# Three attention stages: operand rows loaded in runs of 24, 16 and 8 partitions, and the sums over the values taken once per key tile

## The chip, the cores and the metric

The kernel runs on one core of a Trainium2 chip. Its engines are TensorE (PE, matmuls; PEld its weight loads), VectorE (DVE), ScalarE (ACT), GpSimd (POOL) and SyncE (SP, which here issues all DMAs). The metric is the device time of one execution in microseconds (us), the median of several.

## What is computed

A chain of eight layers on x of 4 x 1024 tokens of 128 features. Three are attentions with 16 heads of 8 features; the others are mixtures of experts, a fast-weight layer and low-rank layers, which the diff does not touch. The three attentions, cut to their core:

```python
# a: linear biases                                   (4 batches, 16 heads, 1024 x 1024 scores)
scores = einsum('bqhd,bkhd->bhqk', q, k) / sqrt(8) + slopes[h] * -abs(i - j)
out = einsum('bhqk,bkhd->bqhd', softmax(scores), v)
# b: scores damped by distance
scores = einsum('bhsd,bhtd->bhst', q, k) / sqrt(8) * exp(-abs(decay) * abs(i - j))
# c: no projection, x minus its mean over time is query and key, x itself the value
corr = softmax(einsum('bthd,bThd->bhtT', xc, xc)); out = einsum('bhtT,bThd->bthd', corr, xh)
```

## The kernel before

**Operands.** Scores are taken from bf16 numbers at nearly f32 precision: each f32 query and key is split into three bf16 parts (0 coarse, 1 middle, 2 fine), and six products of parts are added. So a head's operand has 6 x 8 = 48 rows (`ROWS`), one block of 8 rows for each entry of `Q_PARTS` and `K_PARTS`. The parts are made in `project_qkv` (stages a and b) and `centre_and_split` (c), stored to DRAM in `parts_dram`, and loaded from there into `q_rows` and `k_rows`, four heads (`GH`) side by side. The 48 rows are there twice, at partitions 0 and 64 (`PAIR_ROW`), so that two matmuls of 64 rows run beside each other in PE.

**Loads.** In `attend_transposed` SP loads the operands of a group (one batch, four heads) while the group before it is worked on; `half` is one of two buffers. It waits on `o_out`, the copies of the sums of the group that used the buffer before, and issues one DMA for each block of 8 rows, for k and for q and for both places: 24 DMAs, of 64 KB mostly, and two more for bias rows (a) or shift rows (c).

**The attention's loop.** `attend_transposed` works on 16 groups a stage. A group has 8 key tiles J of 128 keys, a key tile has 4 units (one head each), so 32 units n. For a unit, PE computes a score tile of 128 keys x 1024 queries (`scores`, L741, two matmuls, one for each half c of the queries) into one of 3 slots of PSUM (`SLOTS`). In a and b DVE then adjusts the 512 columns in the half that holds the keys (L831, L828), and signals `adjusted`. ACT takes the exponential of the tile (L804) into `probs`. When all four heads of a key tile are there, PE multiplies the values with them (`sum_up`, L760), into one PSUM bank for each half c; an f32 matmul shows as two instructions in the trace, so one half of a key tile is 8 instructions. At the end of a group DVE copies both banks out (`take_sums`, L817).

**The order on PE** is written out in `batch`: at unit n first `scores` of unit n + 3, which waits until the exponential of unit n has freed the slot, then sums. Half 0 of a key tile is summed at its last unit (n % 4 == 3), half 1 two units later, except for the last key tile of a group, where both are taken at once:

```python
if n % GH == GH - 1:
    sum_up(hg, n // GH, 0, b)
    if n + 1 == UNITS:
        sum_up(hg, n // GH, 1, b)
if n % GH == 1 and n > GH:
    sum_up(hg, n // GH - 1, 1, b)
```

In stage a `alibi_span` leaves out scores far from the diagonal for the heads with steep slopes: heads 0 to 3 keep narrow spans, heads 8 to 15 are full. The function `attend` is another route for wide scores; this execution does not take it.

Of the kernel before, what the change touches and what calls it, by code (L numbers as in the profile page):

```python
# [16 lines left out]
BF16 = mybir.dt.bfloat16  # L17
# [4 lines left out]
D = 128  # L22
BATCH, SEQ = 4, 1024
# [5 lines left out]
CHUNK = 512  # L29
# [151 lines left out]
Q_PARTS = (0, 0, 1, 1, 0, 2)  # L181
K_PARTS = (0, 1, 0, 1, 2, 0)
# [6 lines left out]
def project_qkv(nc, tag, XT, w_qkv, b_qk, b_v, V, parts_dram, scale, head_of, longest2, damp=None):  # L189
# [8 lines left out]
    with ExitStack() as stack:  # L198
# [105 lines left out]
        def _(act):  # L304
            for x in range(SPLITS + 1):
                b = x % RING
                if x < SPLITS:
                    u, v = divmod(x, VERS)
                    act.wait_ge(biased, x + 1)
                    if x >= RING:  # L310
                        act.wait_ge(stored[b], 16 * (x // RING))
                    act.copy(parts[:, b, 0, :], full[:, b, :]).then_inc(part1, 1)
                    if v == 0:
                        if u >= 2 * RING:
                            act.wait_ge(norm2_done, u // 4 - 1)
                        act.activation(squares[:, u % (2 * RING), :], full[:, b, :], ACT.Square).then_inc(squared, 1)
# [13 lines left out]
        def _(sp):  # L330
            for x in range(SPLITS):
# [3 lines left out]
                sp.dma_start(parts_dram[v, w].rearrange("s f t -> f s t")[:, :, c * CHUNK:(c + 1) * CHUNK],  # L335
                             parts[:, x % RING, :, :]).then_inc(stored[x % RING], 16)
            for b in range(RING):
                sp.wait_ge(stored[b], 16 * (SPLITS // RING))
# [68 lines left out]
def attend(nc, tag, V, operands, parts_dram, tables, op, out_all, ident):  # L407
# [7 lines left out]
    with ExitStack() as stack:  # L415
# [36 lines left out]
        def _(sp):  # L452
            with sp.Fori(0, HEADS // GH) as hg:
                with sp.Fori(0, BATCH // 2) as bp:
                    for half in range(2):

                        sp.wait_ge(group_done, hg * 4 + bp * 2 + (half + 1))
                        for rows, which, order in ((q_rows, 0, Q_PARTS), (k_rows, 1, K_PARTS)):
                            for n, part in enumerate(order):
                                src = parts_dram[0, which, part].rearrange("(h e) t -> e h t", e=HD)  # L460
# [183 lines left out]
def attend_transposed(nc, tag, V, operands, parts_dram, out_t, ident, shift_dram=None, table=None, slopes=None,  # L644
# [23 lines left out]
    with ExitStack() as stack:  # L668
# [14 lines left out]
        LOADS = 4 * len(Q_PARTS) + 2 * (bias_dram is not None or shift_dram is not None)  # L683

        @block.sync
        def _(sp):
            with sp.Fori(0, BATCH) as b:
                for hg in range(HG):
                    half, hs, at = hg % 2, slice(hg * GH, (hg + 1) * GH), bass.ds(b * SEQ, SEQ)
                    sp.wait_ge(o_out, b * (2 * HG) + (2 * hg + 2))  # L690
                    for tile in range(2):
                        for n, (qp, kp) in enumerate(zip(Q_PARTS, K_PARTS)):
                            rows = slice(PAIR_ROW * tile + n * HD, PAIR_ROW * tile + (n + 1) * HD)
                            version = far * tile
                            q_src = parts_dram[version, 0, qp].rearrange("(h e) t -> e h t", e=HD)
                            k_src = parts_dram[version, int(by_dve), kp].rearrange("(h e) t -> e h t", e=HD)
                            sp.dma_start(k_rows[rows, half, :, :], k_src[:, hs, at]).then_inc(loaded[half], 16)
                            if by_dve:
                                sp.dma_start(q_rows[rows, half, :, :], q_src[:, hs, at]).then_inc(loaded[half], 16)
                            else:  # L700
                                sp.dma_start(q_rows[rows, half, :, tile * SIDE:(tile + 1) * SIDE],
                                             q_src[:, hs, bass.ds(b * SEQ + tile * SIDE, SIDE)]
                                             ).then_inc(loaded[half], 16)
# [20 lines left out]
        def _(pe):  # L724
# [42 lines left out]
            def batch(b, final):  # L767
                for hg in range(HG):
                    for n in range(UNITS):
# [8 lines left out]
                        if n % GH == GH - 1:  # L778
                            sum_up(hg, n // GH, 0, b)
                            if n + 1 == UNITS:  # L780
                                sum_up(hg, n // GH, 1, b)
                        if n % GH == 1 and n > GH:
                            sum_up(hg, n // GH - 1, 1, b)
# [384 lines left out]
def centre_and_split(nc, tag, XT, parts_dram, shift_dram, head_of):  # L1168


    with ExitStack() as stack:
# [69 lines left out]
        def _(sp):  # L1241
            for b, c in enumerate(cut):
                sp.wait_ge(part3, b + 1)
                sp.dma_start(parts_dram[0, 0].rearrange("s f t -> f s t")[:, :, c], parts[:, :, c]).then_inc(stored, 16)
# [3 lines left out]
            sp.wait_ge(stored, 16 * 2 * BATCH)  # L1248
# [1046 lines left out]
def build(nc, t, out, stages=8, first=0):  # L2295
    with ExitStack() as stack:
# [3 lines left out]
        parts_dram = nc.dram_tensor("qk_parts", [2, 2, 3, D, TOK], BF16, kind="Internal").ap()  # L2300
# [96 lines left out]
```

## Time and profile before

| | |
|---|---|
| median of 3 runs | 3687.84 us (3684.51 to 3689.68) |
| the profiled execution, its own time | 3692.91 us |
| its span, first to last instruction | 3691.2 us |
| PE busy | 2983.0 us (81%) |
| ACT busy | 2362.0 us (64%) |
| DVE busy | 2264.1 us (61%) |
| POOL busy | 471.1 us (13%) |
| mean granted clock of PE | 0.909 |
| DMA | 107.70 MB, mean 29 GB/s |

The busy share of an engine is an average over eight layers with different limits, so a stage has to be read by itself. The stages touched here lie at 126 to 690 us (a), 1372 to 1892 us (b) and 3133 to 3608 us (c). PE's clock has two levels, 1.2 GHz (0.5 in the profile) and 2.4 GHz (1.00).

### The profile page before, as it was taken

To read this page: it belongs to the slowest core of one execution; us is meant where nothing else is said; L and a number is where in the kernel's file an instruction comes from. 1 tells how busy PE (TensorE), PEld (TensorE's weight loads), DVE (VectorE), ACT (ScalarE), POOL (GpSimd) and SP (SyncE) were. 2 spreads that over 40 slices of the span, in tenths; PEclk is the share of its full clock that TensorE was granted. 3 is DMA by queue.
4 is the path that set the end of the run, shared out by engine and by line. 5 is a ranking of instruction groups with operands and counts; after the bars stand their busy time and mean duration, and the time that the engine had idled before them with its cause. 6 is when DMAs were issued, how large, how long until landed. Compare 5 with 4: busy or idle time off the path is not lost. (4 is left out here: it accounts for less than half of the span.)

```text
span 3691.2 us, 56232 instructions
## 1 busy us (share of the span) xinstructions
PE 2983.0 (81%) x18300; PEld 1343.0 (36%) x18300; DVE 2264.1 (61%) x3797; ACT 2362.0 (64%) x3466; POOL 471.1 (13%) x320
## 2 busy tenths in 40 slices
PE   4588888799999438888879999968886842999997
PEld 2111212366666311111136666632235640111115
DVE  6466666677777657666666777767779966000004
ACT  5577777455444539988955544455533344999993
POOL 5000000000000330000000000026544422000002
PEclk9788898899999759999999999989989965999998
DMA  3333434000000143333310000000000002232220
GB/s 99 56 48 45 50 46 51 24 1 0 1 0 0 48 122 46 49 52 48 49 31 1 0 1 0 0 25 1 0 0 0 0 3 55 35 42 42 41 31 25
DMA packets 77585, 107.70 MB, mean 29 GB/s; under 512 B 12224, under 2 KB 42944, under 8 KB 76560
## 3 DMA queue, kind: packets, MB, share of 16 engines
q1 hardware_dynamic: 77392, 105.18, 17.4%
q8 instruction: 115, 1.88, 0.2%
q14 instruction: 78, 0.64, 0.1%
HBM read 80.59 MB, written 24.54 MB: 28 GB/s over the span
## 5 line engine op out<-in xcount | busy, mean ns | idle before, releaser
L804 ACT ACTIVATE a_direct_probs<-a_direct_s_ps 128x1024 f32<-128x1024 f32 (+10 forms) x512 | 432.3, 939 | 153.8 <-DVE a_direct_s_ps L831 115.8
L804 ACT ACTIVATE b_direct_probs<-b_direct_s_ps 128x1024 f32<-128x1024 f32 x512 | 474.8, 1093 | 72.3 <-DVE b_direct_s_ps L828 62.4
L1438 ACT ACTIVATE m_mix_hidden<-m_mix_up_ps 128x512 f32<-128x512 f32 x512 | 305.7, 597 | 295.7 <-PE m_mix_up_ps L1382 295.7
L804 ACT ACTIVATE c_att_probs<-c_att_s_ps 128x1024 f32<-128x1024 f32 x512 | 470.2, 1171 | 22.0 <-PE c_att_s_ps L741 18.9
L831 DVE SCALAR_TENSOR_TENSOR a_direct_s_ps<-a_distance,a_slopes,a_direct_s_ps 128x512 f32<-128x512 f32 (+3 forms) x512 | 354.3, 732 | 197.2 <-PE a_direct_s_ps L741 186.0
L1390 PE MATMUL m_mix_down_ps<-m_w,m_mix_hidden 128*128 128x128 f32 x4096 | 474.8, 276 | 0.0
L1390 PEld LDWEIGHTS m_mix_down_ps<-m_w,m_mix_hidden 128*128 128x128 f32 x4096 | 467.2, 192 | 15.3 <-issue 15.3
L1382 PE MATMUL m_mix_up_ps<-m_mix_ZT,m_w 128*128 128x512 f32 x1024 | 472.1, 619 | 0.0
L828 DVE TENSOR_TENSOR b_direct_s_ps<-b_direct_s_ps,b_distance 128x512 f32<-128x512 f32 x512 | 333.6, 694 | 181.9 <-PE b_direct_s_ps L741 181.9
L817 DVE COPY c_out_t<-c_att_o_ps 128x512 f32 x32 | 20.6, 686 | 478.6 <-PE c_att_o_ps L760 478.6
L741 PE MATMUL a_direct_s_ps<-a_q_rows,a_k_rows 64*128 64x512 bf16 (+12 forms) x984 | 200.8, 399 | 133.1 <-DMA a_k_rows<-bias_rows 70.2
L760 PE MATMUL a_direct_o_ps<-a_direct_probs,a_v_cols 128*32 128x512 f32 (+14 forms) x2168 | 292.7, 598 | 1.0 <-ACT a_direct_probs L804 1.0
L741 PE MATMUL b_direct_s_ps<-b_q_rows,b_k_rows 64*128 64x512 bf16 x1024 | 199.6, 401 | 104.3 <-ACT b_direct_probs L804 40.8
L760 PE MATMUL b_direct_o_ps<-b_direct_probs,b_v_cols 128*32 128x512 f32 x2048 | 280.8, 627 | 1.9 <-ACT b_direct_probs L804 1.6
L760 PE MATMUL c_att_o_ps<-c_att_probs,c_v_cols 128*32 128x512 f32 x2048 | 271.2, 607 | 1.0 <-ACT c_att_probs L804 1.0
L1382 PEld LDWEIGHTS m_mix_up_ps<-m_mix_ZT,m_w 128*128 128x128 f32 x1024 | 157.6, 190 | 291.4 <-ACT m_mix_hidden L1438 274.1
L741 PE MATMUL c_att_s_ps<-c_q_rows,c_k_rows 64*128 64x512 bf16 x1024 | 197.3, 390 | 77.0 <-DMA c_q_rows<-shift 37.3
L1543 DVE TENSOR_REDUCE m_mix_mixed<-m_mix_weighted 128x128 f32<-128x1024 f32 x128 | 246.7, 1927 | 4.4
L741 PEld LDWEIGHTS b_direct_s_ps<-b_q_rows,b_k_rows 64*128 64x128 bf16 x1024 | 46.8, 93 | 388.0 <-ACT b_direct_probs L804 343.1
L1754 POOL TENSOR_TENSOR f_recur_dots_prods<-f_recur_dots_vecs 128x512 f32<-128x512 f32 (+1 forms) x64 | 173.0, 2715 | 105.9 <-DVE f_recur_dots_vecs L1786 105.9
L741 PEld LDWEIGHTS a_direct_s_ps<-a_q_rows,a_k_rows 64*128 64x128 bf16 x984 | 45.8, 95 | 380.4 <-ACT a_direct_probs L804 280.6
L741 PEld LDWEIGHTS c_att_s_ps<-c_q_rows,c_k_rows 64*128 64x128 bf16 x1024 | 47.6, 93 | 357.0 <-ACT c_att_probs L804 315.3
(343 smaller groups left out, 3768.3 us busy)
## 6 DMA issues: line engine op xcount, KB each, us to landing
a_k_rows<-qk_parts SPq DMA_DIRECT2D x192, 64.0 KB
a_q_rows<-qk_parts SPq DMA_DIRECT2D x192, 64.0 KB
qk_parts<-b_qkv_parts SPq DMA_DIRECT2D x32, 384.0 KB, 2.5
b_k_rows<-qk_parts SPq DMA_DIRECT2D x192, 64.0 KB
b_q_rows<-qk_parts SPq DMA_DIRECT2D x192, 64.0 KB
c_k_rows<-qk_parts SPq DMA_DIRECT2D x192, 64.0 KB
qk_parts<-a_qkv_parts SPq DMA_DIRECT2D x16, 384.0 KB, 2.5
c_q_rows<-qk_parts SPq DMA_DIRECT2D x192, 32.0 KB
```

The source lines that it names most:

```text
L741: last = pe.matmul(s_ps[:, slot(hg, n), left:right], k_rows[rows, half, j, J * P:(J + 1) * P], q_rows[rows, half, j, left:right], start=Tr ...
L760: last = pe.matmul(o_ps[VW * j:VW * (j + 1), c, lo - c * BANK:hi - c * BANK], v_cols[:, hg % 2, J, j, :], probs[:, J % 2, j, lo:hi], start ...
L804: act.activation(probs[:, J % 2, j, lo:hi], s_ps[:, slot(hg, n), lo:hi], ACT.Exp).then_inc(exped, 1)
L817: dve.tensor_copy(dst, o_ps[:, c, :]).then_inc(o_out, 1)
L828: ins = dve.tensor_tensor(held, held, near, ALU.mult)
L831: ins = dve.scalar_tensor_tensor(out=held, in0=near, scalar=slopes[:, h:h + 1], in1=held, op0=ALU.mult, op1=ALU.add)
L1382: pe.matmul(up_ps[:, f % UP_BANKS, :], w["w1"][:, f * P:(f + 1) * P], ZT[:, half, :], start=True, stop=True).then_inc(up_done, 1)
L1390: last = pe.matmul(down_ps[:, t % 2, e, :], hidden[:, e * HALVES + h, t * P:(t + 1) * P], w["w2"][:, e * HALVES + h, :], start=(h == 0), s ...
L1438: act.activation(hidden[:, f, :], up_ps[:, f % UP_BANKS, :], ACT.Silu).then_inc(silu_done, 1)
L1543: dve.tensor_reduce(mixed[:, :], weighted[:, :, :].rearrange("p e d -> p d e"), AX, ALU.add).then_inc(summed, 1)
L1754: return engine.tensor_tensor(prods[:, c % 2, at:at + n, :], vecs[:, c % 2, 0:n, :], vecs[:, c % 2, other:other + 1, :].to_broadcast([P, n ...
```

## The change

It has two parts. First, the order of the parts in the operand rows is another one, and `parts_dram` now holds for each head its three parts of 8 rows one after another (for the keys in the reverse order). With that, neighbouring blocks of operand rows are neighbours in DRAM too, so that 3, 2 and 1 blocks come in one DMA (`SLOT_RUNS`): 12 DMAs a group in place of 24. The stores go part by part: three DMAs in place of one for each piece in a and b; in c both orders are stored, 24 DMAs in place of 4 and twice the bytes. Second, both halves of the sums are taken at the last unit of every key tile.

```diff
-Q_PARTS = (0, 0, 1, 1, 0, 2)
-K_PARTS = (0, 1, 0, 1, 2, 0)
+Q_PARTS = (0, 1, 2, 0, 1, 0)
+K_PARTS = (2, 1, 0, 1, 0, 0)
+Q_SLOTS = Q_PARTS
+K_SLOTS = tuple(2 - part for part in K_PARTS)
+SLOT_RUNS = ((0, 3), (3, 2), (5, 1))
...
-                sp.dma_start(parts_dram[v, w].rearrange("s f t -> f s t")[:, :, c * CHUNK:(c + 1) * CHUNK],
-                             parts[:, x % RING, :, :]).then_inc(stored[x % RING], 16)
+                for part in range(3):
+                    slot = 2 - part if w else part
+                    sp.dma_start(parts_dram[v, w, :, slot * HD:(slot + 1) * HD, c * CHUNK:(c + 1) * CHUNK],
+                                 parts[:, x % RING, part, :]).then_inc(stored[x % RING], 16)
...
-        LOADS = 4 * len(Q_PARTS) + 2 * (bias_dram is not None or shift_dram is not None)
+        LOADS = 4 * len(SLOT_RUNS) + 2 * (bias_dram is not None or shift_dram is not None)
...
-                        for n, (qp, kp) in enumerate(zip(Q_PARTS, K_PARTS)):
-                            rows = slice(PAIR_ROW * tile + n * HD, PAIR_ROW * tile + (n + 1) * HD)
-                            version = far * tile
-                            q_src = parts_dram[version, 0, qp].rearrange("(h e) t -> e h t", e=HD)
-                            k_src = parts_dram[version, int(by_dve), kp].rearrange("(h e) t -> e h t", e=HD)
-                            sp.dma_start(k_rows[rows, half, :, :], k_src[:, hs, at]).then_inc(loaded[half], 16)
+                        version = far * tile
+                        q_from = parts_dram[version, 0, hs].rearrange("h r t -> r h t")
+                        k_from = parts_dram[version, 1, hs].rearrange("h r t -> r h t")
+                        for n, count in SLOT_RUNS:
+                            row = PAIR_ROW * tile + n * HD
+                            rows = slice(row, row + count * HD)
+                            q_run, k_run = (slice(at_ * HD, (at_ + count) * HD) for at_ in (Q_SLOTS[n], K_SLOTS[n]))
+                            sp.dma_start(k_rows[rows, half, :, :], k_from[k_run, :, at]).then_inc(loaded[half], 16)
+                            sp.dma_start(q_rows[rows, half, :, cols], q_from[q_run, :, q_at]).then_inc(loaded[half], 16)
...
                         if n % GH == GH - 1:
                             sum_up(hg, n // GH, 0, b)
-                            if n + 1 == UNITS:
-                                sum_up(hg, n // GH, 1, b)
-                        if n % GH == 1 and n > GH:
-                            sum_up(hg, n // GH - 1, 1, b)
+                            sum_up(hg, n // GH, 1, b)
...
-                sp.dma_start(parts_dram[0, 0].rearrange("s f t -> f s t")[:, :, c], parts[:, :, c]).then_inc(stored, 16)
+                for w in range(2):
+                    for part in range(3):
+                        slot = 2 - part if w else part
+                        sp.dma_start(parts_dram[0, w, :, slot * HD:(slot + 1) * HD, c],
+                                     parts[:, part, c]).then_inc(stored, 16)
...
-        parts_dram = nc.dram_tensor("qk_parts", [2, 2, 3, D, TOK], BF16, kind="Internal").ap()
+        parts_dram = nc.dram_tensor("qk_parts", [2, 2, HEADS, 3 * HD, TOK], BF16, kind="Internal").ap()
```

PE in stage b, inside the first group, before: `b_direct_s_ps` are the score slots, `b_direct_o_ps` the banks of the sums.

```order
L734 REGISTER_ALU
L741 MATMUL b_direct_s_ps<-b_q_rows,b_k_rows 128x512 x2
L734 REGISTER_ALU
L741 MATMUL b_direct_s_ps<-b_q_rows,b_k_rows 128x512 x2
L760 MATMUL b_direct_o_ps<-b_direct_probs,b_v_cols 32x512 x4
L734 REGISTER_ALU
L741 MATMUL b_direct_s_ps<-b_q_rows,b_k_rows 128x512 x2
L734 REGISTER_ALU
L741 MATMUL b_direct_s_ps<-b_q_rows,b_k_rows 128x512 x2
L760 MATMUL b_direct_o_ps<-b_direct_probs,b_v_cols 32x512 x4
```

And the same place of the changed kernel:

```order
L739 REGISTER_ALU
L746 MATMUL b_direct_s_ps<-b_q_rows,b_k_rows 128x512 x2
L739 REGISTER_ALU
L746 MATMUL b_direct_s_ps<-b_q_rows,b_k_rows 128x512 x2
L739 REGISTER_ALU
L746 MATMUL b_direct_s_ps<-b_q_rows,b_k_rows 128x512 x2
L739 REGISTER_ALU
L746 MATMUL b_direct_s_ps<-b_q_rows,b_k_rows 128x512 x2
L765 MATMUL b_direct_o_ps<-b_direct_probs,b_v_cols 32x512 x8
```

Four sum matmuls after every second unit have become eight after every fourth.

SP in stage a, at the start of the attention: the first loads of a group before (`a_k_rows` and `a_q_rows` are the operand rows, the sizes partitions x heads x columns).

```order
L697 ISA
L697 DMA a_k_rows<-qk_parts 8x4x1024
L699 REGISTER_ALU
L699 DMA a_q_rows<-qk_parts 8x4x1024
L697 ISA
L697 DMA a_k_rows<-qk_parts 8x4x1024
L699 DMA a_q_rows<-qk_parts 8x4x1024
```

And in the changed kernel:

```order
L707 ISA
L707 DMA a_k_rows<-qk_parts 24x4x1024
L708 REGISTER_ALU
L708 DMA a_q_rows<-qk_parts 24x4x1024
L707 ISA
L707 DMA a_k_rows<-qk_parts 16x4x1024
L708 DMA a_q_rows<-qk_parts 16x4x1024
L707 ISA
L707 DMA a_k_rows<-qk_parts 8x4x1024
L708 DMA a_q_rows<-qk_parts 8x4x1024
```

These six DMAs bring all 48 rows of k and q for one place, which took twelve before.

## Rows read from the trace of the kernel before

**Rows 1.** Busy time: stretch, PE, PEld, DVE, ACT, POOL, PEclk, DMA share, GB/s.

```profile
126.00:690.00 564.00, 462.93 (x3173) 115.00 (x3172) 375.22 (x551) 432.27 (x512) 5.60 (x14) 0.88 0.35 45
1372.00:1892.00 520.00, 446.09 (x3056) 89.03 (x3056) 351.87 (x542) 474.35 (x512) 5.61 (x14) 0.95 0.36 46
3133.00:3608.00 475.00, 433.77 (x3056) 89.16 (x3056) 19.32 (x30) 470.02 (x512) 5.61 (x14) 0.99 0.26 38
```

**Rows 2.** Timeline of b inside a group: start, length in us, engine.

```profile
1410.43 0.39 PE L741 MATMUL b_direct_s_ps<-b_q_rows,b_k_rows 64*128 64x512 bf16 x2 [2.18 <-ACT b_direct_probs L804]
...
1410.75 1.06 PE L760 MATMUL b_direct_o_ps<-b_direct_probs,b_v_cols 128*32 128x512 f32 x8
...
1412.59 1.06 PE L760 MATMUL b_direct_o_ps<-b_direct_probs,b_v_cols 128*32 128x512 f32 x8
...
1413.58 0.91 PE L741 MATMUL b_direct_s_ps<-b_q_rows,b_k_rows 64*128 64x512 bf16 x4
...
1414.01 1.30 DVE L828 TENSOR_TENSOR b_direct_s_ps<-b_direct_s_ps,b_distance 128x512 f32<-128x512 f32 x2 [0.53 <-PE b_direct_s_ps L741]
```

**Rows 3.** Timeline of b where one group ends and the next begins.

```profile
1405.11 0.10 PEld L741 LDWEIGHTS b_direct_s_ps<-b_q_rows,b_k_rows 64*128 64x128 bf16 x2 [0.42 <-ACT b_direct_probs L804]
...
1405.43 1.92 PE L760 MATMUL b_direct_o_ps<-b_direct_probs,b_v_cols 128*32 128x512 f32 x16
...
1407.29 0.96 PE L741 MATMUL b_direct_s_ps<-b_q_rows,b_k_rows 64*128 64x512 bf16 x6
1407.42 1.29 DVE L817 COPY b_out_t<-b_direct_o_ps 128x512 f32<-128x512 f32 x2 [1.10 <-PE b_direct_o_ps L760]
...
1408.63 1.89 DVE L828 TENSOR_TENSOR b_direct_s_ps<-b_direct_s_ps,b_distance 128x512 f32<-128x512 f32 x3
...
1409.36 29.45 ACT L804 ACTIVATE b_direct_probs<-b_direct_s_ps 128x1024 f32<-128x1024 f32 x32 [1.55 <-DVE b_direct_s_ps L828]
```

**Rows 4.** Score tiles of a and b: duration ns min/median/max, starts.

```profile
L831 DVE SCALAR_TENSOR_TENSOR a_direct_s_ps<-a_distance,a_slopes,a_direct_s_ps x512: 506/751/757, 126.2 to 682.2; 128x512 f32<-128x512 f32 x144, 128x280 f32<-128x280 f32 x6, 128x471 f32<-128x471 f32 x6, 128x432 f32<-128x432 f32 x6
...
L828 DVE TENSOR_TENSOR b_direct_s_ps<-b_direct_s_ps,b_distance x512: 689/698/700, 1373.1 to 1890.6; 128x512 f32<-128x512 f32 x171
```

**Rows 5.** Timeline of c at a group's end.

```profile
3165.91 0.10 PEld L741 LDWEIGHTS c_att_s_ps<-c_q_rows,c_k_rows 64*128 64x128 bf16 x2 [0.42 <-ACT c_att_probs L804]
...
3166.24 1.92 PE L760 MATMUL c_att_o_ps<-c_att_probs,c_v_cols 128*32 128x512 f32 x16
...
3168.09 0.96 PE L741 MATMUL c_att_s_ps<-c_q_rows,c_k_rows 64*128 64x512 bf16 x6
```

**Rows 6.** Timeline of ACT in a's first group.

```profile
133.30 1.80 ACT L804 ACTIVATE a_direct_probs<-a_direct_s_ps 128x686 f32<-128x686 f32 x3 [1.76 <-DVE a_direct_s_ps L831]
...
137.96 1.81 ACT L804 ACTIVATE a_direct_probs<-a_direct_s_ps 128x814 f32<-128x814 f32 x3 [1.68 <-DVE a_direct_s_ps L831]
```

**Rows 7.** Timeline of a: first operand load, first scores.

```profile
97.19 0.40 SPq L697 DMA_DIRECT2D a_k_rows<-qk_parts  x1
...
125.78 1.06 PE L741 MATMUL a_direct_s_ps<-a_q_rows,a_k_rows 64*128 64x280 bf16 x3 [34.70 <-DMA a_k_rows<-bias_rows]
```

**Rows 8.** Busy time by stretch during a's first load.

```profile
100.00:105.00 5.00, 0.00 (x0) 0.00 (x0) 0.00 (x0) 0.00 (x0) 0.00 (x0) 0.50 0.55 66
```

**Rows 9.** Waits of PE for loads in stages a, b, c: total, times, longest.

```profile
PE a_direct_s_ps L741 <- DMA a_k_rows<-bias_rows: 35.5, 13, 4.2
...
PE b_direct_s_ps L741 <- DMA b_q_rows<-qk_parts: 37.3, 6, 32.3
...
PE c_att_s_ps L741 <- DMA c_q_rows<-shift: 37.3, 1, 37.3
```

**Rows 10.** Busy time by stretch while c's parts are stored.

```profile
3100.00:3105.00 5.00, 0.00 (x0) 0.00 (x0) 4.89 (x5) 3.79 (x5) 0.00 (x0) 0.50 1.03 379
```

**Rows 11.** Busy time by stretch at a start of group, and after one.

```profile
333.00:341.00 8.00, 5.17 (x38) 1.10 (x38) 6.37 (x11) 6.63 (x8) 0.40 (x1) 1.00 0.42 56
1505.00:1520.00 15.00, 13.57 (x82) 2.35 (x82) 8.85 (x15) 12.81 (x15) 0.00 (x0) 0.77 0.54 70
```

More of the change, by code:

```diff
@@ L310, in _ @@
                     if x >= RING:
-                        act.wait_ge(stored[b], 16 * (x // RING))
+                        act.wait_ge(stored[b], 16 * 3 * (x // RING))
                     act.copy(parts[:, b, 0, :], full[:, b, :]).then_inc(part1, 1)
@@ L334, in _ @@
                 sp.wait_ge(part3, x + 1)
-                sp.dma_start(parts_dram[v, w].rearrange("s f t -> f s t")[:, :, c * CHUNK:(c + 1) * CHUNK],
-                             parts[:, x % RING, :, :]).then_inc(stored[x % RING], 16)
+                for part in range(3):
+                    slot = 2 - part if w else part
+                    sp.dma_start(parts_dram[v, w, :, slot * HD:(slot + 1) * HD, c * CHUNK:(c + 1) * CHUNK],
+                                 parts[:, x % RING, part, :]).then_inc(stored[x % RING], 16)
             for b in range(RING):
-                sp.wait_ge(stored[b], 16 * (SPLITS // RING))
+                sp.wait_ge(stored[b], 16 * 3 * (SPLITS // RING))
 PAIR_ROW = 64
@@ L457, in _ @@
                         sp.wait_ge(group_done, hg * 4 + bp * 2 + (half + 1))
-                        for rows, which, order in ((q_rows, 0, Q_PARTS), (k_rows, 1, K_PARTS)):
-                            for n, part in enumerate(order):
-                                src = parts_dram[0, which, part].rearrange("(h e) t -> e h t", e=HD)
+                        for rows, which, order in ((q_rows, 0, Q_SLOTS), (k_rows, 1, K_SLOTS)):
+                            for n, slot in enumerate(order):
+                                src = parts_dram[0, which, :, slot * HD:(slot + 1) * HD].rearrange("h e t -> e h t")
                                 sp.dma_start(
@@ L691, in _ @@
                     for tile in range(2):
-                        for n, (qp, kp) in enumerate(zip(Q_PARTS, K_PARTS)):
-                            rows = slice(PAIR_ROW * tile + n * HD, PAIR_ROW * tile + (n + 1) * HD)
-                            version = far * tile
-                            q_src = parts_dram[version, 0, qp].rearrange("(h e) t -> e h t", e=HD)
-                            k_src = parts_dram[version, int(by_dve), kp].rearrange("(h e) t -> e h t", e=HD)
-                            sp.dma_start(k_rows[rows, half, :, :], k_src[:, hs, at]).then_inc(loaded[half], 16)
[L698 to L703, printed above, removed]
+                        version = far * tile
+                        q_from = parts_dram[version, 0, hs].rearrange("h r t -> r h t")
+                        k_from = parts_dram[version, 1, hs].rearrange("h r t -> r h t")
+                        cols, q_at = slice(0, SEQ), at
+                        if not by_dve:
+                            cols, q_at = slice(tile * SIDE, (tile + 1) * SIDE), bass.ds(b * SEQ + tile * SIDE, SIDE)
+                        for n, count in SLOT_RUNS:
[4 more added lines that the diff above has]
+                            sp.dma_start(q_rows[rows, half, :, cols], q_from[q_run, :, q_at]).then_inc(loaded[half], 16)
                         if shift_dram is not None:
@@ L1247, in _ @@
                 sp.dma_start(shift_dram[:, c], shift[:, c]).then_inc(stored, 16)
-            sp.wait_ge(stored, 16 * 2 * BATCH)
+            sp.wait_ge(stored, 16 * 7 * BATCH)
 GROUPS, PER_GROUP = 4, 2
```

## The prediction

> **What bounds the kernel now.** I read the busy table of the page first: no engine is above 81%, so the time is a sum of stages with different limits. Then the busy time by stretch for the three attention stages, because the diff touches only these and what feeds them. They take 564, 520 and 475 us of 3691 [rows 1]. In c ScalarE (ACT, the exponentials) is busy 470 of 475 us: it is the bound, and nothing else counts. In b it is 474 of 520, in a 432 of 564; there the reader should see that ACT still leads but that something keeps interrupting it.
>
> The timeline of b says how. Inside a group TensorE (PE) scores units two ahead of sums and takes a half of the sums after every second unit: halves start at 1410.75 and 1412.59, 1.83 apart, so a key tile of four units takes 3.67 us [rows 2]. ACT's row of 32 exponentials takes 29.45 us, 0.92 each or 3.67 for four [rows 3]. The two paces are equal: ACT never starves, but with no slack.
>
> The three score slots are the slack. Unit n+3 can be scored when exponential n is done; the sums of a key tile also wait for exponential n. Whatever PE does between scores n+3 and scores n+4 must be over before ACT has emptied the slots n+1 to n+3, and in a and b VectorE (DVE) must have adjusted unit n+4 as well.
>
> **The sums, back to back: the main term.** The change puts 8 matmuls in place of 4 at the end of a key tile and none two units later (the order of PE below the diff). The kernel before already does exactly this at one place, the last key tile of each group, so the trace shows the price. In b scores n+3 start at 1405.11, released by ACT; both halves start at 1405.43 and block PE; scores n+4 start at 1407.29 [rows 3]: 2.18 us. Behind them every unit needs the adjustment and the exponential. Scores at 1413.58 are followed by DVE at 1414.01: 0.43 [rows 2]. DVE at 1408.63 is followed by ACT at 1409.36: 0.73 [rows 3]. ACT at 1409.36 releases scores at 1410.43: 1.07 [rows 3, 2]. That closes the loop, from one scores n+3 to the next: 2.18 + 0.43 + 0.73 + 1.07 = 4.41 us a key tile. It no longer depends on ACT's own pace (3.67), so each tile costs 0.74 more. I leave the output copies out of this sum; they start at 1407.42, take 1.29 and delay the adjustment only at a group's end [rows 3], where nothing changes.
>
> - b: 16 groups of 7 inner tiles, 112 x 0.74 = 83 us.
> - a, heads 8 to 15 (full width): 56 tiles. The adjustment takes 0.751 against 0.698 us [rows 4], so the loop is 4.46 and a tile costs 0.80: 45 us. Heads 4 to 7: 28 tiles; head 7, whose exponential carries the loop, is full width, so 0.80 again: 22 us.
> - a, heads 0 to 3: narrow spans; here a tile already takes 4.66 us at 1.2 GHz, from 133.30 to 137.96, with ACT waiting 1.7 of it [rows 6]. The same serial loop appears, with shorter terms. Not shown by any row; between 0 (PE does the same work) and 1.1 a tile (b's 0.74 made half longer by the slow clock) I take 0.7, near the full heads because the wait for DVE is already there: 20 us (0 to 30).
> - c: no adjustment, so 2.18 + 0.43 (PE to ACT, taken like PE to DVE) + 1.07 = 3.68, with 2.18 between 3165.91 and 3168.09 [rows 5]. ACT alone needs 3.67. Cost 0.01 a tile, 2 us: hidden by ACT's own work. Without that cover it would be b's.
>
> **The clock.** After a group's end PE's granted clock falls in some groups: 0.77 over 1505 to 1520, that is partly 1.2 instead of 2.4 GHz [rows 11]; the mean is 0.88 in a and 0.95 in b [rows 1]. A loop with more idle PE time recovers later. At 1.2 GHz the 1.86 us of sums become 3.7 and the loop about 6.5. I allow 15 us, bounds 0 and 40 (a further microsecond at each of some 32 groups).
>
> **The loads.** Now 24 loads of 8 partitions (64 KB) bring a group's operands; then 12, of 24, 16 and 8. Bytes are the same. In a the first is issued at 97.19 and the first scores start at 125.78, 28.6 us [rows 7]. The transfers set it: 66 GB/s at a DMA share of 0.55, 8.8 of 16 engines, and no engine computes [rows 8]. The stores of c, over 128 partitions, reach 379 GB/s at 1.03 [rows 10]. So the narrow runs waste engines. Bounds: no gain (the rate stays at 66), or 200 GB/s, half of the store's, which brings 26 us of transfer down to 9. I take 0.6 of the time, nearer the old row because a third of the DMAs keep 8 partitions: 28.6 to 18, -10 us in a; in b, whose first wait is 32.3 [rows 9], with two loads fewer, -9; in c, whose q rows are half as long and whose wait holds some 19 us of transfer, -7. Sum -26 (0 to -48).
>
> The Trainium skill ("DMA: Bandwidth & Descriptors", the part on how many engines a DMA uses) says that a DMA runs on the largest number up to 16 that divides the slowest dimension of both sides: 8 for 8 rows, 12 for 24, 16 for 16. The trace's 8.8 agrees for 8 rows. By that rule the busiest engine would carry 16 packets where it carried 24, two thirds of the time, -23 us, almost my number.
>
> Inside the stages PE waited 13 times more for loads in a, 35.5 us, and in b 5.0 beside the first [rows 9]. A faster load ends them, and so would the slower groups by themselves, since a group then lasts 36 us or more against 28 of load. -38 us in all, taken whole: PE's wait holds back the sums queued behind it, for which ACT waits.
>
> **The stores.** One DMA of parts becomes three, same bytes, in a and b. Two issues more of 0.40 each [rows 7] are hidden between the splits; behind the last split they show, 1 us in each stage. In c bytes double (the queries' version is written in both orders): 3.1 MB more at 379 GB/s is 8 us. What hides them is DVE's work on the shifts, 4.89 of 5 us in the same stretch [rows 10], which the attention needs too; without that cover all 8 would show. I take +1. Sum +3 (0 to 10). The new order of parts in the rows changes no count of products.
>
> **Sum.** 83 + 45 + 22 + 20 + 2 + 15 - 26 - 38 + 3 = +126 us. The profiled execution took 3692.9 (span 3691.2, 1.7 around it), 5 above the median 3687.8. Forecast for the median: 3687.8 + 126 = 3814, rounded to 3815.
>
> **Rivals.**
> 1. *The stall at a tile is hidden; only the loads count: faster.* Place: PE between scores n+3 and n+4. If the loop closes within 3.67 us, 3688 - 26 - 38 + 3 = 3627. For it: PE saves a switch between kinds of matmul per tile, 0.14 us (two halves apart take 2 x 1.00, together 1.86) [rows 2, 3]. Against: the loop is summed from the kernel's own rows, and 0.74 is missing. The gains of 61 us are used up at 0.31 us over 196 tiles of full width, so it decides at a loop of 3.98. Chance 0.06, and 0.02 for a tie there.
> 2. *The loads gain nothing.* If 66 GB/s is a limit of the source and not of the eight partitions, the first waits stay: 3814 + 26 = 3840. For it: both tiles read the same rows of memory, 8 KB apart, as before. Chance 0.15.
> 3. *The clock stays low.* With PE idle about a quarter of every tile, the slow level could hold for half of the stages: 196 tiles x 2.1 x 0.5 = +206, 4020. Against it: PE was idle more than a third of 333 to 341, and its clock stayed at 1.00 [rows 11]. Chance 0.05. [...]
> 4. That the change does not do what it says is excluded for the order of PE and the shape of the loads by the listings of instructions.
>
> **Chances and range.** The forecast has 0.72, no gain in the loads 0.15, the clock 0.05, faster 0.06, a tie 0.02. Low end: the forecast with -48 for the loads, 0 for clock and narrow heads: 3757. High end: loads at 0, clock 40, stores 10, narrow heads 30: 3880. That covers the first two. A measurement of this kernel tells some 0.2% (7 us) from no change: slower by more than that 0.92, within it 0.02, faster 0.06.
>
> **What would show it.** In the new trace of b, rows of 16 sum instructions every 4.4 us, ACT idle 0.7 us before one of four exponentials with DVE as releaser, stage b near 600 us; c within 5 us of 475. First load in a 18 us. No waits of PE for loads inside a. The prediction is wrong if b's tile stays near 3.7, or if PEclk in a and b falls well below 0.88.

## The result: 3.1% slower

The changed kernel takes 3802.6 us (median of 4 runs, 3795.5 to 3820.9), the kernel before 3688.8 beside it (4 runs): a ratio of 1.0312 (95% interval 1.0269 to 1.0354). The profiled execution has a span of 3793.8 us, 102.6 more than before, and a mean granted clock of 0.925 (before 0.909).

The page of the changed kernel, engines first:

```profile
PE 2860.5 (75%) x18300; PEld 1354.7 (36%) x18300; DVE 2247.4 (59%) x3797; ACT 2374.5 (63%) x3466; POOL 460.5 (12%) x320
```

Every engine has about the work it had (PE 2860.5 us busy for 2983.0, ACT 2374.5 for 2362.0). So the extra time is idle time. The three attention stages say where it lies (busy time by stretch, columns as in [rows 1]):

```profile
126.00:706.00 580.00, 395.71 (x3128) 116.74 (x3127) 366.11 (x537) 432.26 (x508) 5.60 (x14) 0.95 0.32 43
1393.00:1995.00 602.00, 417.29 (x3048) 94.53 (x3046) 348.11 (x539) 480.68 (x510) 5.61 (x14) 0.96 0.29 39
3238.00:3708.00 470.00, 398.91 (x3040) 92.11 (x3042) 19.34 (x30) 468.27 (x509) 5.61 (x14) 0.99 0.25 37
```

Measured in the timelines, the 102.6 us are ("last exponential" means its end):

| part of the span | before | after | difference |
|---|---|---|---|
| start to a's first operand load | 97.19 | 102.94 | +5.7 |
| first load to first exponential: a, b, c | 29.67, 27.94, 19.82 | 21.15, 20.41, 14.78 | -8.5, -7.5, -5.0 |
| first to last exponential: a | 557.2 | 584.5 | +27.3 |
| b | 518.5 | 604.4 | +85.9 |
| c | 473.6 | 474.1 | +0.4 |
| b's end to c's first operand load | 1222.3 | 1226.4 | +4.1 |
| everything else | | | +0.2 |

Stage b is the heart of it. Its timeline inside a group, where [rows 2] show the kernel before:

```profile
1422.20 3.77 ACT L806 ACTIVATE b_direct_probs<-b_direct_s_ps 128x1024 f32<-128x1024 f32 x4 [0.65 <-DVE b_direct_s_ps L830]
...
1423.28 0.39 PE L746 MATMUL b_direct_s_ps<-b_q_rows,b_k_rows 64*128 64x512 bf16 x2 [1.28 <-ACT b_direct_probs L806]
...
1423.60 1.92 PE L765 MATMUL b_direct_o_ps<-b_direct_probs,b_v_cols 128*32 128x512 f32 x16
...
1425.45 0.96 PE L746 MATMUL b_direct_s_ps<-b_q_rows,b_k_rows 64*128 64x512 bf16 x6
...
1425.89 1.90 DVE L830 TENSOR_TENSOR b_direct_s_ps<-b_direct_s_ps,b_distance 128x512 f32<-128x512 f32 x3 [1.48 <-PE b_direct_s_ps L746]
...
1426.62 3.77 ACT L806 ACTIVATE b_direct_probs<-b_direct_s_ps 128x1024 f32<-128x1024 f32 x4 [0.65 <-DVE b_direct_s_ps L830]
```

The rows of 16 sum instructions stand where rows of 8 stood. Walk the loop: scores n+3 at 1423.28, sums at 1423.60, scores n+4 at 1425.45, DVE at 1425.89, ACT at 1426.62. From ACT row to ACT row it is 4.42 us, and in each round ACT stands idle 0.65 us with DVE as the releaser. In a the same loop takes 4.48 us (the median over the tiles of heads 4 to 15). Before, ACT ran all 32 units in one row [rows 3]. In c, where DVE is not in the loop, the same 16 sum instructions leave ACT without a gap:

```profile
3258.99 9.31 ACT L806 ACTIVATE c_att_probs<-c_att_s_ps 128x1024 f32<-128x1024 f32 x10
3260.07 0.39 PE L746 MATMUL c_att_s_ps<-c_q_rows,c_k_rows 64*128 64x512 bf16 x2 [0.55 <-ACT c_att_probs L806]
3260.39 1.92 PE L765 MATMUL c_att_o_ps<-c_att_probs,c_v_cols 128*32 128x512 f32 x16
...
3263.75 0.39 PE L746 MATMUL c_att_s_ps<-c_q_rows,c_k_rows 64*128 64x512 bf16 x2 [0.55 <-ACT c_att_probs L806]
```

Two scores rows in the same place of the loop are 3.68 us apart (3260.07 to 3263.75), the pace of ACT itself.

The loads did get faster. Busy time by stretch during a's first load, against a DMA share of 0.55 and 66 GB/s in [rows 8], and then PE's waits for loads in the whole run, against [rows 9]: one in each stage, the first, and none inside.

```profile
108.00:113.00 5.00, 0.00 (x0) 0.00 (x0) 0.00 (x0) 0.00 (x0) 0.00 (x0) 0.50 0.92 130
```

```profile
PE c_att_s_ps L746 <- DMA c_q_rows<-shift: 38.3, 1, 38.3
...
PE a_direct_s_ps L746 <- DMA a_k_rows<-bias_rows: 25.9, 1, 25.9
PE b_direct_s_ps L746 <- DMA b_q_rows<-qk_parts: 24.7, 1, 24.7
```

### The profile page after: what moved, and what is told of

It reads as the page before. It is cut to its first block and busy times, and to the rows that moved or that the text cites. A ratio compares the mean times of both kernels' runs of the same rounds, so it can differ in the third digit from the quotient of the medians.

```text
span 3793.8 us, 55084 instructions
## 1 busy us (share of the span) xinstructions
PE 2860.5 (75%) x18300; PEld 1354.7 (36%) x18300; DVE 2247.4 (59%) x3797; ACT 2374.5 (63%) x3466; POOL 460.5 (12%) x320
## 5 line engine op out<-in xcount | busy, mean ns | idle before, releaser
L806 ACT ACTIVATE b_direct_probs<-b_direct_s_ps 128x1024 f32<-128x1024 f32 x512 | 483.1, 1030 | 141.6 <-DVE b_direct_s_ps L830 141.6
L806 ACT ACTIVATE c_att_probs<-c_att_s_ps 128x1024 f32<-128x1024 f32 x512 | 472.3, 1030 | 15.3 <-PE c_att_s_ps L746 14.9
L746 PE MATMUL b_direct_s_ps<-b_q_rows,b_k_rows 64*128 64x512 bf16 x1024 | 176.0, 393 | 206.2 <-ACT b_direct_probs L806 177.8
L746 PE MATMUL a_direct_s_ps<-a_q_rows,a_k_rows 64*128 64x512 bf16 (+13 forms) x984 | 170.5, 377 | 210.8 <-ACT a_direct_probs L806 183.1
L765 PE MATMUL b_direct_o_ps<-b_direct_probs,b_v_cols 128*32 128x512 f32 x2048 | 262.7, 633 | 4.8 <-ACT b_direct_probs L806 4.8
L746 PE MATMUL c_att_s_ps<-c_q_rows,c_k_rows 64*128 64x512 bf16 x1024 | 174.2, 387 | 109.7 <-ACT c_att_probs L806 71.4
L765 PE MATMUL a_direct_o_ps<-a_direct_probs,a_v_cols 128*32 128x512 f32 (+15 forms) x2168 | 247.4, 553 | 1.9 <-ACT a_direct_probs L806 1.9
L765 PE MATMUL c_att_o_ps<-c_att_probs,c_v_cols 128*32 128x512 f32 x2048 | 247.4, 601 | 1.1 <-ACT c_att_probs L806 1.1
L1546 DVE TENSOR_TENSOR m_mix_weighted<-m_mix_down_ps,m_mix_combine 128x1024 f32<-128x1024 f32 x128 | 156.4, 1222 | 30.2 <-PE m_mix_down_ps L1396 24.6
```

The costliest lines, as they stand in the source:

```text
L746: last = pe.matmul(s_ps[:, slot(hg, n), left:right], k_rows[rows, half, j, J * P:(J + 1) * P], q_rows[rows, half, j, left:right], start=Tr ...
L765: last = pe.matmul(o_ps[VW * j:VW * (j + 1), c, lo - c * BANK:hi - c * BANK], v_cols[:, hg % 2, J, j, :], probs[:, J % 2, j, lo:hi], start ...
L806: act.activation(probs[:, J % 2, j, lo:hi], s_ps[:, slot(hg, n), lo:hi], ACT.Exp).then_inc(exped, 1)
L1546: dve.tensor_tensor(weighted[:, :, :], down_ps[:, t % 2, :, :], over(combine[:, half, t, :], D), ALU.mult).then_inc(down_out, 1)
```

## The experiments

All ratios are to the kernel before, run on the same chip beside them, with 95% intervals. "Attention" is the time from a stage's first exponential to the end of its last, in the one profiled execution of each run. It varies a little where nothing in the stage was changed. With new loads and the old order of the sums b takes 521.9 us in the loads alone and 510.3 to 514.8 in six other runs. In the five of these runs without a stall or waits for loads inside a, a takes 492.1 to 498.5.

### The two parts apart

The loads alone: the changed kernel with the old order of the sums.

```diff
                         if n % GH == GH - 1:
                             sum_up(hg, n // GH, 0, b)
-                            sum_up(hg, n // GH, 1, b)
+                            if n + 1 == UNITS:
+                                sum_up(hg, n // GH, 1, b)
+                        if n % GH == 1 and n > GH:
+                            sum_up(hg, n // GH - 1, 1, b)
```

> The runs of 24, 16 and 8 rows and the new layout, with the sums in the old places. Main theory: the loss of the changed kernel is all in the sums, and the loads gain by themselves. First scores some 21 us after the first load's issue in a and b (28.6 before), no waits of PE for loads inside a; stage a falls from 557 us by some 33, b by 5, c stays at 474; the first loads give 21 us, the stores take 10. In all 3689 - 49 = 3640 us, ratio 0.987. Rival theory, that loads inside a were never what held ACT and vanished only because groups got longer: only first loads and stores count, 3689 - 11 = 3678.

The sums alone: the kernel before with both halves at `n % GH == GH - 1`.

> The kernel before with both halves of the sums at each key tile's last unit; loads and layout as before. Main theory (a serial loop over PE, DVE and ACT): a key tile of b takes 4.41 us, stage b about 605 us, a about 585, c 474; first loads as before. In all the changed kernel without its 11 us from loads and stores: 3814 us, ratio 1.034. Rival, that the loss comes from the new order of parts or the new loads in some way: below 3750.

Measured: loads alone 3616.0 us, ratio 0.9799 (0.9776 to 0.9822); sums alone 3817.8, ratio 1.035 (1.0331 to 1.0369). So the change is a good part and a bad part. The bad part came as expected. The good part was worth 73 us where I had given it 49, and the surplus is in a: its attention fell from 557.2 to 492.1 us, 65 us (59 to 65 by the other runs with these loads), though the waits for loads inside it add up to 35.5 [rows 9]. Busy time of a's attention with the loads alone:

```profile
124.00:613.00 489.00, 420.64 (x3130) 107.78 (x3129) 368.68 (x539) 427.21 (x508) 5.63 (x14) 0.96 0.38 51
```

ACT has the same work as in [rows 1]; its idle time there went from 132 to 62 us (564.00 less 432.27; 489.00 less 427.21), and PE did the same work in 42 us less, at a clock of 0.96 in place of 0.88.

The two parts do not add up: -73 and +128 make +55, and the change as a whole costs 114. With the new order of the sums a group of b lasts 36 us or more and a load of 28 us is never late, so the load waits vanish whether the loads are faster or not (sums alone: one wait for loads a stage). Behind slow sums the fast loads are worth little: 15 us by the medians (3817.8 less 3802.6), though the runs of the two overlap, and 8 by the profiled spans (3801.7 less 3793.8). Behind fast sums they are worth 73.

### Eight sum matmuls in a row in c alone

The loads alone, with both halves at once only where `not by_dve`.

> As the first of these four, but in stage c both halves of the sums at each key tile's last unit; a and b sum as before. Main theory: without the adjustment on DVE the loop closes in 3.68 us against 3.67 of ACT, so c takes 474 to 476 us, the whole the same as the first within 0.1%. Rival, that eight sum matmuls in a row cost by themselves (0.74 a tile): c at 557 us, the whole 83 us slower.

Measured 3618.1 us, ratio 0.9811 (0.9792 to 0.9831), the same as the loads alone; c's attention 473.7 us. A block of eight is not bad in itself.

### Is VectorE's adjustment in the loop?

```diff
                 left, right = max(lo, side * SIDE), min(hi, (side + 1) * SIDE)
...
+                right = left + 64
```

> The kernel before with the new order of the sums, and in a and b VectorE adjusts only 64 of the 512 columns of each score tile (so its output is not the reference's; everything else runs). My theory: a key tile of b is the closed loop scores -> VectorE -> ScalarE -> scores with 2.18 us of sums in it (2.18 + 0.43 + 0.73 + 1.07 = 4.41). With VectorE's term down from 0.73 to 0.2 to 0.3 us, the loop is 3.88 to 3.98 us: b's 112 inner key tiles lose about 50 us against the same order with the full adjustment (b 604 -> about 550 us), a's 56 + 28 full tiles about 35 (a 589 -> about 555), c stays at 474: some 3730 us in all. Rival (TensorE's own work and clock set the new pace, not the chain through VectorE): b and a stay at 604 and 589, 3815 us.

> Control for the run with the short adjustment: the kernel before, old order of the sums, only the adjustment cut to 64 of 512 columns (output not the reference's). My theory: with the old order VectorE's term lies beside the sums, ScalarE alone sets the inner key tile (3.67 us), so the cut is worth little: b stays within 10 us of 518, total 3665 to 3690 us; what moves is at the ends of the groups (4 x 0.5 us a stage). Rival (VectorE's adjustment is on the path in both orders): b loses some 50 us here too, total about 3600.

Measured: with the new order 3694.8 us, ratio 1.0022 (1.0002 to 1.0042); with the old one 3683.4, ratio 0.9973 (0.9954 to 0.9991). By the medians the same cut is worth 123 us in one order and 4 in the other (3 to 17 by the interval). In b 60 us went with the new order (attention 543.8, for some 550 expected), and 7 with the old (511.7), no more than b varies without a change. In a 58 went with the new order (530.7), more than the 35 expected, and with the old it grew by 6 (562.9). There PE's waits for loads inside the stage grew from 35.5 to 66.2 us, so the control says nothing about a. The pair can be read in b. The timeline of b with the new order and the short adjustment:

```profile
1433.26 3.77 ACT L801 ACTIVATE b_direct_probs<-b_direct_s_ps 128x1024 f32<-128x1024 f32 x4 [0.18 <-DVE b_direct_s_ps L826]
...
1436.52 0.96 PE L741 MATMUL b_direct_s_ps<-b_q_rows,b_k_rows 64*128 64x512 bf16 x6
1436.95 0.80 DVE L826 TENSOR_TENSOR b_direct_s_ps<-b_direct_s_ps,b_distance 128x64 f32<-128x64 f32 x3 [1.94 <-PE b_direct_s_ps L741]
1437.22 3.77 ACT L801 ACTIVATE b_direct_probs<-b_direct_s_ps 128x1024 f32<-128x1024 f32 x4 [0.18 <-DVE b_direct_s_ps L826]
```

DVE to ACT is 0.27 us here (1436.95 to 1437.22) in place of 0.73, and the loop 3.96 in place of 4.42: both fell by 0.46. That shows the loop with VectorE in it. TensorE's work, the same in both, does not set the pace alone.

### One scores step between the halves

```diff
                         if n % GH == GH - 1:
                             sum_up(hg, n // GH, 0, b)
-                            sum_up(hg, n // GH, 1, b)
+                            if n + 1 == UNITS:
+                                sum_up(hg, n // GH, 1, b)
+                        if n % GH == 0 and n >= GH:
+                            sum_up(hg, n // GH - 1, 1, b)
```

> The new loads, and the second half of the sums one unit after the first (one scores step between them) in place of two units (before) or none (the change). My theory: what costs is that 1.86 us of sums stand in one piece between two scores steps; with one scores step in between, a walk of the loop by the rows of before gives 3.73 us a key tile (old 3.63 to 3.67, new 4.41): b 521 to 535 us, total 3616 to 3645. Rival (the second half is taken earlier than before, and any earlier place waits on ScalarE's last exponential and holds the scores up): halfway or more of the cost, b 560 us or more, total 3700 or more.

Measured 3666.7 us, ratio 0.9935 (0.9909 to 0.9962), attention in b 540.5 and in a 526.1. It fell between the two expectations. In b it lies 19 us over the loads alone, and 26 to 30 over the other runs with these loads; the change lies 82, and 90 to 94, over them. In a it costs 28 to 34 us. In b, from the third key tile of a group on, the starts of the exponentials alternate, 4.04 us for one key tile and 3.67 for the next. My walk gave 3.73; the mean of 3.86 costs 0.19 a tile over 3.67, a quarter of the 0.74 of the full block, and more than my walk had. Of the places tried, only the old one, two steps behind the first half, costs nothing; why one of two tiles is late was not followed up.

### What makes the loads faster

Everything of the loads alone, but every run cut into single blocks: `SLOT_RUNS = tuple((n, 1) for n in range(6))`. And then in runs of 16, 8, 16 and 8: `SLOT_RUNS = ((0, 2), (2, 1), (3, 2), (5, 1))`.

> As the first of these four, but the rows loaded in runs of 8 again, 24 DMAs a group, from the new layout. If the length of the run, and with it the number of DMA engines, makes the loads faster, the first scores are back at 28 to 29 us behind the first issue and PE waits inside a for some 35 us; with 10 us for the stores 3699 us, ratio 1.003. If the layout in DRAM makes them faster, it stays at 21 us and the time near 3640.

> The new loads with the old order of the sums, but the run of 24 partitions cut into 16 and 8, so that there are runs of 16, 8, 16 and 8 (16 load instructions a group in place of 12). My theory (few DMA engines work on a run of 8 partitions; runs of 16 reach them all): the busiest engine carries as much as before, so the first loads take what they take with 24, 16 and 8 (20 to 22 us in a, 20 to 22 in b, 15 in c), total 3610 to 3630 us. Rival (the number of load instructions decides, each with a fixed cost on the queue): four more instructions of 24 saved of before's 48 or so add a sixth to a third of the gain back, first loads 23 to 26 us in a and b, total 3630 to 3650.

Measured: single blocks 3694.2 us, ratio 1.0016 (1.0000 to 1.0032); 16/8/16/8 3627.4, ratio 0.9822 (0.9786 to 0.9858). First load to first exponential in a, b and c:

| runs | a | b | c | DMAs a group |
|---|---|---|---|---|
| 8 (kernel before) | 29.7 | 27.9 | 19.8 | 24 |
| 8, new layout | 29.9 | 27.8 | 18.9 | 24 |
| 16, 8, 16, 8 | 25.3 | 23.8 | 17.7 | 16 |
| 24, 16, 8 | 20.3 | 22.0 | 15.0 | 12 |

So the layout in DRAM gives nothing; cutting the rows into fewer and longer runs does. The column of a has to be read with care: with the loads of the kernel before it is 23.1 in the sums alone and 25.3 in the short adjustment with the new order. In the sums alone the DMA share is as before (0.54), at 80 GB/s in place of 66; why is open. b and c agree better: runs of 8 take 27.1 to 27.9 in b and 18.9 to 20.8 in c over five profiles, 24/16/8 takes 19.9 to 22.4 and 14.5 to 16.4 over eight.

For 16/8/16/8 my theory of the first loads (20 to 22 us) failed: in its one profile they lie between the two others in all three stages, as the rival said (23 to 26 in a and b). The total does not tell the two apart: 3627.4 lies in the range of the theory (3610 to 3630), and the interval of its ratio overlaps that of the loads alone. Busy time by stretch of 16/8/16/8, 5 us behind a's first load issue as in the line of the changed kernel above (single blocks: a share of 0.54 and 66 GB/s):

```profile
108.00:113.00 5.00, 0.00 (x0) 0.00 (x0) 0.00 (x0) 0.00 (x0) 0.00 (x0) 0.50 1.06 118
```

The DMA share is higher (1.06) than with 24/16/8 in the changed kernel (0.92), for fewer bytes a second (118 against 130). A share over 1 also shows that this measure, the time of all packets over 16 engines, is no strict count of engines at work. Busy engines are not the same as bytes moved. Whether the number of DMAs or the mix of their lengths costs the rest was not separated.

### Where the other 30 us of stage a went

Two runs ask whether a gap costs more than it lasts. First a stall by ScalarE, with a semaphore that keeps the three copies in order:

```diff
...
+                    for i in range(3 if idle is not None else 0):
+                        act.wait_ge(idled, b * (3 * HG) + (3 * hg + i + 1))
+                        act.copy(idle[:, :], table[:, 0:SEQ]).then_inc(idled, 1)
                     for n in range(UNITS):
```

> The new loads with the old order of the sums, and in a alone ScalarE makes three copies of 1024 columns that nobody reads before the first exponential of each of the 16 groups (work added, output the same), so TensorE runs dry for some 3.3 us at each group's start, about as long as a wait for a load inside a of the kernel before (35.5 us in 13). Question: the loads alone took 65 us from a's attention, but TensorE's waits for loads add up to only 35. My theory: each such gap also costs TensorE's clock (0.88 granted in a of the kernel before, 0.95 to 0.99 with the new loads), and the tiles behind it are slower. Then a is 492 + 15 x 3.3 = 541 us and 15 to 30 us more, 556 to 575, with the granted clock of a below 0.92. Rival (a gap costs what it lasts; the other 30 us came from elsewhere in the loads, such as transfers beside the attention): 536 to 546 us, clock above 0.94.

Measured 3646.1 us, ratio 0.9889 (0.9857 to 0.9920); a's attention 525.0, clock 0.91. Neither number: both theories added the stall to ACT's time, but ACT had idle time of its own at the start of a group, which took in part of it. The copies made ACT busy for 45 us more and a is 33 longer. By unit of the group, ACT's idle time before the first four exponentials fell by 25 us, and before the 28 behind them it grew by 12 (32 to 44). In the kernel before it is 42 there. So tiles behind a group's start that come late account for 10 to 12 of the 30 us. Whether the clock makes them late this run does not separate. PE waited for no load inside, and its own longest gap was no longer than in the loads alone (2.4):

```profile
PE a_direct_s_ps L748 <- ACT a_direct_probs L816: 66.5, 99, 2.3
```

Then late loads, with transfers as fast as before:

```diff
-                    sp.wait_ge(o_out, b * (2 * HG) + (2 * hg + 2))
+                    if hg and bias_dram is not None:
+                        sp.wait_ge(exped, b * NB + ((hg - 1) * UNITS + 10 + SLOTS))
+                    else:
+                        sp.wait_ge(o_out, b * (2 * HG) + (2 * hg + 2))
```

> The new loads with the old order of the sums; in a, SyncE issues the loads of groups 1, 2 and 3 of each batch only after the 10th exponential of the group in progress, so that 12 of them come a few us too late, as in the kernel before, though each transfer is as fast as with the change. Question left by the run with the stall on ScalarE (a: 525 us, 33 more than without for 47 us of copies; clock 0.90): does a wait of TensorE for a load cost more than it lasts? My theory: yes, since TensorE falls behind in the order of its own instructions and the tiles behind it come late (in the kernel before ScalarE's idle time fell by 39 us at the first unit of the groups and by 25 us at the next ones). With TensorE waiting W us for loads in a (I expect 25 to 40), a grows over 492 by 1.5 W or more, to 535 to 560 us. Rival (the slow transfers themselves, 8 partitions at a time beside the attention, slow a down, not the waits): a grows by W alone, 517 to 532 us.

The control holds them only until the 4th exponential:

> Control for the late loads: the same hold, after the 4th exponential in place of the 10th. The transfer takes some 20 us and 25 units (23 us) are left, so no wait for a load is expected. Both theories: a 490 to 498 us, total 3612 to 3625. If a is over 505 us without waits for loads, the hold itself costs and the run beside it can't be read as one on waits.

Measured: control 3615.1 us, ratio 0.9801 (0.9785 to 0.9818), a's attention 496.6, no wait for a load inside. Late loads 3656.8, ratio 0.9924 (0.9899 to 0.9950), a's attention 535.5. Waits of PE for loads, then busy time, in a's attention of the run with late loads; last the busy time of the control:

```profile
PE a_direct_s_ps L749 <- DMA a_k_rows<-bias_rows: 20.8, 11, 3.1
```

```profile
124.00:656.00 532.00, 442.92 (x3129) 109.19 (x3129) 369.53 (x538) 429.07 (x508) 5.60 (x14) 0.91 0.37 48
```

```profile
124.00:618.00 494.00, 424.99 (x3131) 107.61 (x3130) 369.11 (x539) 428.00 (x509) 5.64 (x14) 0.95 0.40 52
```

The waits came out shorter than the 25 to 40 us expected. 20.8 us of waits cost 38.9 us against the control, 1.9 for one (1.8 to 2.1 with the other runs without late loads as the base). In the kernel before it was 59 to 65 for 35.5, 1.7 to 1.8 for one. So the rival, that slow transfers beside the attention cost something of their own, is not needed: late loads with fast transfers cost about the same per microsecond. Against the control ACT's idle time grew by 27 us at the first unit of the groups, by 6 at the next three and by 4 behind them. How much of that is the clock (PE 18 us longer for the same work) and how much the order of PE's instructions, where the sums of the finished group stand behind the waiting scores, stays open.

### The stores sooner

```diff
-                sp.wait_ge(part3, x + 1)
-                for part in range(3):
+                for part, ready in enumerate((part1, part2, part3)):
+                    sp.wait_ge(ready, x + 1)
```

The same in `centre_and_split`, with the loop over parts outside that over batches.

> The new loads with the old order of the sums, and each of the three parts stored as soon as it is ready (SyncE waits for part 1, 2 and 3 one by one), where the change waits for part 3 and then issues all three. My theory: the stores' cost is that they are issued late and at 0.6 to 0.7 us each; in c all but the last eight then lie beside the work on parts 2 and 3 and on the shift, so c's way to its first load gets its 4 us back (1226 -> 1222); in a the queue of SyncE is full anyway (45 issues without a gap), so a gets only what an earlier start gives, 1 to 3 us of its 4.6 (101.8 -> 99 to 101). Total 5 to 7 us less than the loads alone: 3609 to 3611 us. Rival (the number of issues and of packets counts, not when they are issued): both stay where they are, 3616 us.

Measured 3610.2 us (5 runs), ratio 0.9803 (0.9777 to 0.9828). a's first load is issued at 96.8 us in place of 101.8, more than expected. For c the way from b's end to the first load does not show the cost (1222.3 here, 1222.1 in the loads alone, 1226.4 in the change), since the layers between vary by more. From the first instruction that makes c's parts to c's first load it is 30.3 us in place of 35.3, and 30.3 in the kernel before. So both are back to before. The total does not show it: the median is 5.8 us below the loads alone, but the kernel before, run beside it, was lower by 4 too (3685.5 for 3689.4), and the ratios are the same (0.9803 and 0.9799). The new loads with the old order of the sums beat both kernels, with early stores or without.

## Why the prediction was right

The forecast was 3815 us with a loop of 4.41; the runs gave 3802.6 and 4.42. The mechanism of the main term was right; several of the smaller terms were not, and their errors partly cancelled. Point by point, by its own steps:

- **The sums, back to back.** Right in mechanism and size. The fair base is the loads alone, where nothing waits for a load inside a stage. Against it b costs 82.5 us (forecast 83), c 0.4 (2), a 92.3 (87). That b agrees to 1 us is luck: by the other runs with these loads b costs 90 to 94 and a 86 to 91. The loops are the firmer evidence: 4.42 us in b for 4.41, 4.48 in heads 4 to 15 of a for 4.46. By heads in a, all batches together: heads 0 to 3 18.8 (20), 4 to 7 25.2 (22), 8 to 15 48.2 (45). The term for the narrow heads was an interpolation and held. The short adjustment shows that the loop goes through VectorE, and c that without it nothing is lost.
- **The clock.** Mis-sized: 15 forecast, nothing seen. PEclk is 0.95 in a and 0.96 in b where it was 0.88 and 0.95 [rows 1]. In the loads alone it is 0.96 and 0.94. The gaps of 1.28 us before the scores of each tile did not lower it. The Trainium skill ("TensorE: Matmul & The Clock Gate", HAM oscillation) describes a kernel that loses the clock in every tile, with waits of some 3 to 5 us between its tiles. The gaps here are shorter, and in this trace it did not happen. The waits for loads held a's clock down: late loads alone took it from 0.95 to 0.91. They are not the only thing that can, since the stall on ScalarE (0.91) and the half one step later (0.92) lowered it with no wait for a load inside a.
- **The first loads.** -21.0 for -26: the share of time kept was 0.71 to 0.75, not 0.6. By the rule of the Trainium skill ("DMA: Bandwidth & Descriptors", how many engines a DMA uses) the busiest engine carries as much with 16/8/16/8 as with 24/16/8. If that set the time, the two would load equally fast. Here 16/8/16/8 took 23.8 us in b against 19.9 to 22.4, and 17.7 in c against 14.5 to 16.4, so the rule does not decide the time alone.
- **The waits inside the stages.** Mis-sized, the largest miss: 38 forecast in all (its rows, 35.5 and 5.0, make 40.5), 59 to 65 measured in a alone, because a wait was costed at what it lasts. In b the loads alone gave nothing certain (521.9, and 510 to 515 in other runs, for 518.5).
- **The stores.** +9.8 for +3. The step that failed is "hidden between the splits", with the price of an issue, written down at 0.40 from a row of loads. The rows of the stores in the changed kernel, duration in ns:

```profile
L340 SPq DMA_DIRECT2D qk_parts<-a_qkv_parts x48: 538/600/1047, 56.8 to 93.5; - x48
```

```profile
L1249 SPq DMA_DIRECT2D qk_parts<-c_split_parts x24: 582/715/1005, 3198.6 to 3216.4; - x24
```

  In a 48 issues of 0.60 and the gaps between them fill SP's queue: it waits for parts 14.0 us in place of 32.3. Of the 5.7 us in a only 1.4 lie behind the last part (11.5 us from it to the first load for 10.1); most of the rest comes before it, among the parts. In c the 24 issues take 18 us, and 19.6 us lie between the last part and the first load where it was 14.9. In b nothing shows (80.4 us from the first part to the first load for 80.6).
- **The sum.** Measured less forecast: +3 for the sums (175 for 172, against the loads alone), -24 for the waits inside (-65 in a and +3 in b for -38), +5 first loads, +7 stores, -15 clock. That is -24, and leads from +126 to the 102.6 us of the profiled pair. The medians beside each other differ by 113.8. The misses have both signs, so the total (3802.6 for 3815) is better than its terms, and that part is luck. The loop of b, 4.42 for 4.41, stands by itself.
- **The rivals.** Rival 1 (the stall hidden) needed a loop under 3.98 and fell. Rival 2 (loads gain nothing) fell: 130 GB/s where it was 66. Rival 3 fell with PEclk.

## What to carry to other kernels

Before work is gathered into one block on an engine, walk the loop that the block stands in, from the wait that frees a slot back to the same wait, with the rows of the trace; it costs next to nothing while the loop is no longer than the busiest engine's own pace (c: 3.68 against 3.67) and all of the difference when it is longer (b: 4.42). Expect a wait of an engine that others wait for to cost more than it lasts when the loop has no slack: in stage a some 1.7 to 2.1 for one. And time the parts of a change apart: here -73 and +128 stood in one diff, and made +114 together.

## What was not expected of the hardware

- A store DMA of one part of a piece takes SP longer to issue than one of all three parts did: 0.600 us against 0.372 in a and b, 0.715 against 0.394 in c (medians). The two differ in pattern as well as in size, and which of it counts was not tried.
- 5 us behind a's first load issue, a DMA share of 1.06 went with 118 GB/s with runs of 16 and 8, and 0.92 with 130 GB/s with runs of 24, 16 and 8. Runs of 8 went with 0.55 and 66.
- Copies of some 3 us on ScalarE at each of 16 group starts took PE's granted clock in a from 0.96 to 0.91, though PE's longest gap inside a was 2.3 us with them and 2.4 without. Gaps of 1.28 us in every key tile left it at 0.95.
